# Attention, feed-forward and next-batch projections: from three stages to pieces dealt out between the products of each attention step

## The reference, cut to what matters

```python
# x: (16, 1024, 256), 16 heads of 16 dims; each of the 16 batches stands alone
q, k, v = split_heads(x @ Wq.T + bq), split_heads(x @ Wk.T + bk), split_heads(x @ Wv.T + bv)
scores = einsum('hbnd,hbmd->hbnm', k, q) / 16
attn   = softmax(scores, axis=-1)
out    = einsum('hbnm,hbmd->hbnd', attn, v)
x = layernorm(x + merge_heads(out) @ Wo.T + bo)
gate, up = x @ (w_gate/127).T, x @ (w_up/127).T          # 768 hidden
x = layernorm(x + (silu(gate) * up) @ (w_down/127).T)
```

## Time and profile before

| | |
|---|---|
| median of three runs | 3302.1 us |
| the profiled execution | 3300.9 us |
| its span, first to last instruction | 3299.1 us |
| PE busy | 2933.6 us, 89% |
| ACT busy | 2502.9 us, 76% |
| DVE busy | 1474.3 us, 45% |
| POOL busy | 564.5 us, 17% |
| granted TensorE clock, mean | 0.951 of 2.4 GHz |
| DMA | 145.9 MB, 44 GB/s |

### The profile page before, as it was taken

The page is one execution under the profiler, slowest core; times in us unless marked ns, Lnnn a source line. Parts: engine busy times, 40 slices in busy tenths (PEclk is TensorE's granted clock), DMA queues, the critical chain, the costliest instruction groups (busy, mean ns, idle before and its releaser), DMA issues.

```text
span 3299.1 us, 54053 instructions
## 1 busy us (share of the span) xinstructions
PE 2933.6 (89%) x17577; PEld 1016.6 (31%) x17608; DVE 1474.3 (45%) x2715; ACT 2502.9 (76%) x3013; POOL 564.5 (17%) x672
## 2 busy tenths in 40 slices
PE   4888989898898998989989998898989889898897
PEld 2224142331423324233242422314223142332413
DVE  3344452444534435353453625445344453443535
ACT  1787869778596785968869687795977969678695
POOL 1103021030210203012030210302103021020302
PEclk7999999999999999999999999999999999999998
DMA  3211102011111111111111011110211111111100
GB/s 104 66 37 46 50 31 66 22 57 39 37 60 34 50 34 50 47 34 57 35 49 50 24 61 33 47 50 31 66 34 45 39 47 50 33 50 34 37 21 14
DMA packets 80224, 145.90 MB, mean 44 GB/s; under 512 B 27584, under 2 KB 30272, under 8 KB 75584
## 3 DMA queue, kind: packets, MB, share of 16 engines
q1 hardware_dynamic: 79808, 140.46, 13.2%
HBM read 88.48 MB, written 50.33 MB: 42 GB/s over the span
## 4 chain that ended last, share of the span: by engine, by line
issue 75%; POOL 13%; PE 7%; ACT 3%; DVE 1%; POOLq 1%; DMA 0%; DVEq 0%; SPq 0%; ACTq 0%
PE psum L991 6%; POOL probs L485 6%; POOL squares L452 4%; ACT probs L556 3%; POOL rstd L466 2%; POOL ln_bias L469 1%; PE psum L994 0%; DMA bo_all<-in_L_attn_bo 0%; POOLq L442 0%; POOL xmax_all L443 0%; DVE inv L815 0%; POOL norm_all L459 0%; POOLq L484 0%; DVE wmax L944 0%; ACT parts L520 0%
## 5 line engine op out<-in xcount | busy, mean ns | idle before, releaser
L556 ACT ACTIVATE probs<-psum 128x1024 f32<-128x1024 f32 x2048 | 1973.7, 1026 | 247.8 <-PE psum L991 225.7
L991 PE MATMUL psum<-probs,v 128*32 128x512 f32 x8192 | 1121.7, 622 | 51.5 <-DVE pv L799 49.6
L991 PE MATMUL psum<-kstack,qstack 51*128 51x512 f16 x4096 | 792.6, 398 | 144.4 <-ACT probs L556 102.9
L991 PEld LDWEIGHTS psum<-kstack,qstack 51*128 51x128 f16 x4096 | 193.8, 93 | 1388.3 <-ACT probs L556 981.9
L715 DVE SCALAR_TENSOR_TENSOR parts<-psum,scale_now,parts 128x512 f16<-128x512 f32 x128 | 96.0, 750 | 822.4 <-ACT parts L520 822.4
L991 PEld LDWEIGHTS psum<-probs,v 128*32 128x32 f32 x8192 | 164.8, 109 | 326.7 <-issue 228.8
L452 POOL TENSOR_TENSOR squares<-parts 128x512 bf16<-128x512 f16 x128 | 133.3, 1041 | 771.4 <-DVE parts L715 771.4
L534 ACT ACTIVATE x_res<-x_res,ln_bias,rstd 128x256 f32<-128x256 f32 x256 | 139.9, 596 | 163.0 <-POOL ln_bias L469 163.0
L466 POOL TENSOR_TENSOR rstd<-vareps,minus_half 128x2 f32<-128x2 f32 x128 | 89.3, 698 | 995.8 <-DVE neg_mean L852 995.8
L485 POOL TENSOR_TENSOR probs<-h,probs 128x512 f16<-128x512 f32 x192 | 222.5, 1159 | 196.9 <-ACT probs L592 196.9
L991 PE MATMUL psum<-outT,gateT 128*128 128x512 f16 x768 | 210.7, 399 | 40.2 <-issue 38.8
(11 more groups left out here) (115 smaller groups left out, 2199.9 us busy)
## 6 DMA issues: line engine op xcount, KB each, us to landing
parts_dram<-parts SPq DMA_DIRECT2D x64, 512.0 KB, 2.8
qstack<-parts_dram SPq DMA_DIRECT2D x384, 64.0 KB, 2.1
kstack<-parts_dram SPq DMA_DIRECT2D x384, 64.0 KB, 2.1
x_pre<-in_L_attn_x SPq DMA_DIRECT2D x17, 1024.0 KB, 5.0
x_res<-in_L_attn_x SPq DMA_DIRECT2D x16, 1024.0 KB, 4.8
out<-x_res SPq DMA_DIRECT2D x32, 512.0 KB, 2.7
kstack<-shift_parts SPq DMA_DIRECT2D x384, 4.0 KB, 1.8
probs<-in_L_ffn_w_gate SPq DMA_DIRECT2D x1, 768.0 KB, 9.0
```

The lines of the kernel that those rows point to most:

```text
L556: nc.scalar.activation(probs[:, k % 2, 2 * pr:2 * pr + 2, hf * HALF:(hf + 1) * HALF], scores[u % 2], ACT.Exp, scale=score_scale).then_inc( ...
L991: return nc.tensor.matmul(o, lhsT, rhs, start=start, stop=stop)
```

## The change

The two stages become one. A batch has now 64 steps (4 groups x 2 halves of 512 columns x 8 tiles) of two units each. Per step PE issues, in this order: the two score pairs, the products of the step before (one half, 4 matmuls), and then *pieces* of items. The items of a middle batch b are the whole preparation of batch b+1 (`xT`, `qk`, `norm`, `v`) and the whole of what was `post` of batch b-1 (`out`, `x1T`, `gate`, `up`, `down`), 60 items in a fixed order (`FULL`). `Plan` deals their matmuls to the 64 steps in proportion to a table `COST` (matmuls and ns of each kind). Batch 0 has only the preparation items, batch 15 only the post items of batch 14, and a tail does those of batch 15 alone. `v`, the scales and the softmax scale are doubled by the batch's parity, so the loop body is two batches.

PSUM: banks 0-3 scores, 4-5 accumulators, now one per segment (group, half), 6-7 the ring for all items. The feed-forward has no longer four banks but these two. PE waits at an item's first piece until the item two places before is emptied.

Emptying: everything by DVE, except the first half of `qk` (ACT `hi`, then DVE) and of `gate` (ACT tanh, then DVE). ACT does these extras of step k after both exponentials of step k: for an item that ended in step e, in step e+1. DVE also takes over `xT`, `v`, the fp16 copy in `x1T`, and the four `normalise`. `take_segment` replaces `take_group`: a 32x32 block transpose of the accumulator on DVE, a reciprocal of 128 x 16, a multiplication, and for every odd group a transpose back.

`decide` stands at step 55 and the flag is read by PE at step 57. POOL reduces the maxima at step 55, after the `rstd` of down 2.

The diff, cut to its core:

```diff
-UNITS = HEADS * TILES
-STEPS = GROUPS * TILES
+STEPS = GROUPS * HALVES * TILES
+UNITS = 2 * STEPS
+RINGS = 2
+ACCS = 2
+COST = {"xT": (4, 109), "x1T": (4, 109), "qk": (2, 868), "norm": (1, 216), "v": (4, 434), "out": (4, 434),
+        "gate": (4, 216), "up": (4, 216), "down": (24, 108)}
+FULL = (some("xT", 0, 1, 2, 3) + some("qk", 0, 1, 2, 3) + some("out", 0, 1, 2, 3) + some("qk", 4, 5)
+        + some("norm", 0, 1, 2, 3) + some("x1T", 0, 1) + gate_up(0, 1, 2, 3) + some("x1T", 2, 3)
+        + gate_up(4, 5, 6, 7, 8, 9, 10, 11) + some("qk", 6, 7) + some("norm", 4, 5) + some("down", 0)
+        + some("norm", 6, 7) + some("down", 1, 2, 3) + some("v", 0, 1, 2, 3))
+DECIDE, RELOAD = 55, 57
+class Plan:
+    def __init__(self, items, prepares):
...
+        for n, (kind, _) in enumerate(items):
+            count, cost = COST[kind]
+            steps = [min(STEPS - 1, (at + cost * i + cost // 2) * STEPS // total) for i in range(count)]
...
+            k = max(k, self.ends[n] + (2 if kind in ("qk", "gate") else 1))
+            self.dve[k].append((kind, j, n))
+            if kind == "qk":
+                self.act[self.ends[n] + 1].append((kind, j, n))
+                self.pool[k].append((kind, j, n))
+            elif kind == "gate":
+                self.act[self.ends[n] + 1].append((kind, j, n))
...
 # ACT
+                for k in range(STEPS):
+                    for pr in range(2):
+                        act.wait_ge(scores_ready, UNITS * b + 2 * k + pr + 1)
+                        if pr == 0 and (k >= 2 or not first):
+                            act.wait_ge(pv_done, STEPS * b + k - 1)
+                        nc.scalar.activation(probs[:, k % 2, 2 * pr:2 * pr + 2, :], scores[pr], ACT.Exp,
+                                             scale=score_scale[par]).then_inc(probs_ready, 1)
+                    extras(k)
 # DVE
+            def take_segment(b, s):
...
+                dve.wait_ge(pv_done, STEPS * b + TILES * (s + 1))
+                nc.vector.transpose(flipped[:, hf, :], bank[ACC + s % ACCS]).then_inc(acc_free, 1)
+                dve.drain()
+                nc.vector.reciprocal(inv[:, hf, :], in_block[:, hf, :, sums])
+                dve.drain()
+                nc.vector.tensor_tensor(scaled_block[:, hf, :, at:at + HEAD_DIM], in_block[:, hf, :, at:at + HEAD_DIM],
+                                        inv[:, hf, :].unsqueeze(2).to_broadcast([P, BLOCKS, HEAD_DIM]), ALU.mult)
+                if odd:
+                    dve.drain()
+                    nc.vector.transpose(outT[:, c, hf * HALF:(hf + 1) * HALF], scaled[:, hf, :]).then_inc(out_ready, 1)
 # PE
+            def do_item(plan, n, lo, hi, start, pre, post, w_parts, fresh=False):
+                kind, j = plan.items[n]
+                o = bank[RING + n % RINGS]
+                count = COST[kind][0]
+                if lo == 0 and not (fresh and n < RINGS):
+                    pe.wait_ge(ring_free, start + n - RINGS + 1)
...
+            def batch(b, par, first, last, w_parts):
+                plan = PRE_PLAN if first else POST_PLAN if last else FULL_PLAN
+                for k in range(STEPS):
+                    if k == RELOAD and not last:
+                        pe.wait_ge(flag_ready, b + 2)
+                    score(b, k, first)
...
+                    if k:
+                        products(b, par, k - 1, first)
...
+                    for n, lo, hi in plan.pieces[k]:
+                        do_item(plan, n, lo, hi, base(b), b + 1, b - 1, w_parts)
+            def everything(w_parts):
+                batch(0, 0, True, False, w_parts)
+                with pe.Fori(1, BATCHES - 1, 2) as b:
+                    batch(b, 1, False, False, w_parts)
+                    batch(b + 1, 0, False, False, w_parts)
+                batch(BATCHES - 1, 1, False, True, w_parts)
+                products(BATCHES - 1, 1, STEPS - 1, False)
+                for n in range(len(ONLY_POST)):
+                    do_item(POST_PLAN, n, 0, COST[ONLY_POST[n][0]][0], base(BATCHES - 1) + len(ONLY_POST), None,
+                            BATCHES - 1, w_parts)
```

More of the change, by code:

```diff
@@ L94 @@
 STACK = ROWS + SHIFT_ROWS
-UNITS = HEADS * TILES
-STEPS = GROUPS * TILES
-PREPARE = 4
+STEPS = GROUPS * HALVES * TILES
+UNITS = 2 * STEPS
+SEGMENTS = GROUPS * HALVES
+PER_GROUP = HALVES * TILES
 QK = 8
[L105 to L110, removed]
@@ L142, in taken @@
[L142 to L161, removed]
@@ new lines, in batch, with extras @@
+            def batch(b, par, first, last):
+                plan = PRE_PLAN if first else POST_PLAN if last else FULL_PLAN
+                def extras(k):
+                    for kind, j, n in plan.act[k]:
+                        if kind == "qk":
+                            hi(j, n, base(b), b + 1, 1 - par)
+                        elif kind == "gate":
+                            tanh(plan, j, n, base(b))
+                        else:
+                            h_hi(j, n, base(b))
+                for k in range(STEPS):
[6 more added lines that the diff above has]
+                    extras(k)
+                    if k == ESC_LOAD and not last:
+                        load_scale(1 - par)
+                for k in range(STEPS, len(plan.act)):
+                    extras(k)
@@ new lines, in _ @@
+            act.wait_ge(scale_ready, 1)
+            load_scale(0)
+            for j in range(QK):
+                hi(j, FIRST.index(("qk", j)), 0, 0, 0, True)
+            batch(0, 0, True, False)
+            with act.Fori(1, BATCHES - 1, 2) as b:
+                batch(b, 1, False, False)
+                batch(b + 1, 0, False, False)
+            batch(BATCHES - 1, 1, False, True)
+            start = base(BATCHES - 1) + len(ONLY_POST)
+            for g in range(2 * HCHUNKS):
+                tanh(POST_PLAN, g, POST_PLAN.place("gate", g), start)
+                if g >= 1:
+                    h_hi(g - 1, POST_PLAN.place("up", g - 1), start)
@@ L897, in batch @@
[L897 to L910 removed]
+                at, sums = odd * HEAD_DIM, (1 - odd) * HEAD_DIM
```

892 lines of the change are left out of this document (367 added, 525 removed).

## The result

The changed kernel takes 3698.9 us (median of four runs, 3687.7 to 3706.1), the kernel before 3299.7 beside it: 1.121 times as long, 95% interval 1.119 to 1.123. The forecast was 3605, within 3200 to 3760. The sign and the mechanism came out, and the amount was 94 us short. All medians here are of executions in the usual state; one of the six of experiment 12's kernel, 4456.1 us at a mean clock of 0.555, is left out.

The account below looks back on a forecast made before the run. The prediction took PE as the bound. Work 171.8, waits 42.1, loop end 1.0 and clock 10 made 224.9 us per middle batch; 14 of these plus 456 us of ends gave 3605 us, range 3200 to 3760.

Parts of the forecast that it names:

- PE's work at full clock: Middle batch: attention steps 103.7 us plus item pieces 68.1 us, 171.8 us of matmuls if nothing waited.
- ring waits, gate stage: Steps 22 to 42: PE waits for gate banks to be emptied, some behind take_segment, 23.9 us per middle batch.
- other waits: Steps 0, 19, 20, 38, 46 and 49: PE waits for copies, norms and extras, 13.4 us per middle batch.
- flag: Before step 57's scores: PE waits behind POOL's reduction and DVE's compare, 4.8 us per middle batch.
- loop end: Loop end every two batches costs some 2 us of issue, 1.0 us per batch.
- the clock: Middle batch: PE's work slows at 1.2 GHz around waits, 10 us taken from between 0 and 17.
- the twelve steps: Steps 22 to 42: each loses 1.3 to 2.05 us to a gate or x1T bank wait, 20.7 us together.
- The transposes: DVE in take_segment: 0.7 us taken from the shuffle's row, bounds 0.5 and 1.4, skill-based estimate 1.24.
- rival with full clock: Whole kernel: same waits, but the array stays at 2.4 GHz, giving 3465 us; chance 0.22.
- cold gate stage: Steps 19 to 49: low clock throughout, unstalled steps 4.9 instead of 2.7 us, giving 3844 us; chance 0.17.
- rival of covered waits: Middle batches: ACT and DVE empty the ring earlier; half covered 3169 us, all 2875; chances 0.14 and 0.04.
- The ends: Outside the middle batches: start 96.8, batch 0 136, batch 15 152, tail 71 us, together 456 us.

Follow-up runs that it names:

- experiment 12: Changed kernel with three ring banks, one accumulator, both POOL reductions earlier, another item order, tanh before the exponentials, flag read at step 58: 3032.5 us, ratio 0.919.
- Experiment 1: Changed kernel with ACT's tanh of gate items moved ahead of the step's two exponentials: 3573.9 us, ratio 1.083.
- experiment 2: Changed kernel with three ring banks and one accumulator bank instead of two and two: 3301.4 us, ratio 1.000.
- Experiment 11: Changed kernel with one accumulator bank, ring of two, plus useless matmuls ahead of nine ring waits: 3640.8 us, ratio 1.105; without these matmuls 3705.5 us.
- experiment 10: Changed kernel's two ring and two accumulator banks, with both POOL reductions earlier, another item order and tanh before the exponentials: 3401.6 us, ratio 1.031.

## Why the prediction was right, and where it was short

By its own steps, for a middle batch:

| | predicted | measured |
|---|---|---|
| PE's work at full clock | 171.8 | 172.6 |
| ring waits, gate stage | 23.9 | 21.1 |
| other waits | 13.4 | 11.7 |
| flag | 4.8 | 4.5 |
| loop end | 1.0 | 1.9 |
| the clock | 10 | 17.0 |
| batch | 224.9 | 228.8 |

The measured waits are PE's idle time between the two flag loads, divided by 14; step 28's wait of about 1.0, which the list puts down to an `x1T` copy, is with the ring waits, where the prediction has it. For the work, the same matmuls in the fastest kernel (experiment 12) serve as the measure:

```profile
229.30:2776.70 2547.40, 2441.94 (x15317) 764.75 (x15319) 1089.41 (x2284) 1958.80 (x2240) 467.35 (x461) 0.99 0.15 48
```

That is 174.4 us busy per batch at a clock of 0.99, so some 1.8 us of it are still from the low clock, and 172.6 is left. The changed kernel's 189.4 is 16.8 above that; with rounding, 17.0 closes the table. The granted clock gives nearly the same: 0.93 over 228.8 us is 14% of it, 32 us, at the lower level, and 16 us lost if all of that falls on work.

**The work** was right: 172.6 against 171.8, and experiment 12's kernel, at 182.0 per batch, comes near it. One reading beside it was not: PE's idle time before was put down mostly to layernorm and the flag, but its list of waits has the exponentials first (102.9 us, "issue" 73.0, the accumulators at the flag 49.6, layernorm 35.8). Nothing in the sum hangs on it.

**The ring waits** came out as counted: +3.67 us of the step, the twelve steps, and the longer waits behind `take_segment` (2.73 and 3.05). Experiment 1 shows that they need the tanh's place and experiment 2 that they need the ring of two. The sum is 2.8 us too high: step 33, behind the longest wait, lost only 0.70 and step 28 only 1.02, less than the 1.3 counted for the shortest, and step 40's even segment was done nearly when its tanh was, so that it waited 1.53, no longer than steps without one.

**The transposes.** The changed kernel shows 0.72 us for 128x512, as I took from the shuffle's row:

```profile
L783 DVE STREAM_TRANSPOSE flipped<-psum 128x512 f32<-128x512 f32 x128 | 91.7, 716 | 326.6 <-PE psum L897 326.4
```

The Trainium skill, page "VectorE: DVE Perf Modes", section "The three transpose paths", led to an estimate of 1.24 us, four times its figure for 128x128 in bf16, which is also for 32x32 blocks. The measurement decides: 0.72 for 128x512 fp32.

**The flag.** The chain stood as predicted, and took the place of the 3.12 of the earlier trace rows. The prediction's own terms add up to 9.4 us from the start of step 55, not to its 9.9; measured, PE goes on at +9.6:

```profile
1370.62 0.37 POOL L441 PARTITION_ALL_REDUCE norm_all<-norm_safe  x1 [5.92 <-issue]
...
1371.37 0.16 DVE L735 TENSOR_TENSOR flag<-over,scales 128x1 int32<-128x1 f32 x1
...
1371.67 1.03 PE L897 MATMUL psum<-kstack,qstack 51*128 51x512 f16 x4 [4.30 <-DVE flag L735]
```

**The clock is the term that was mis-sized.** I took 10 out of 0 to 17, arguing that half of the low stretches lie inside the waits. They hardly do: the low clock comes behind a wait and covers the work there. In the wait of step 32 the granted clock (third from the end) is still 1.00, and in the products behind it 0.50:

```profile
1284.00:1285.30 1.30, 0.00 (x0) 0.00 (x0) 1.27 (x2) 0.00 (x0) 0.00 (x0) 1.00 0.54 136
1287.00:1288.00 1.00, 1.00 (x8) 0.20 (x8) 1.00 (x1) 0.56 (x1) 0.00 (x0) 0.50 0.00 0
```

(In the kernel before, the clock fell inside the wait of 3.12: it is 0.50 in the last 0.9 us of it.) The 34 us of low clock were forecast well (32 measured), and they cost 16 to 17 us, the upper end; 7 more than I took are 98 us in all. Experiment 11 shows 6.1 of them directly, at nine waits; the rest rests on the granted clock and on the comparison with experiment 12. The length of a wait does not alone say what follows: behind 2.12 us in step 26 the next products took 1.06 us, behind 1.88 in step 27 they took 1.94:

```profile
1259.46 1.04 PE L897 MATMUL psum<-ffn,gateT 128*128 128x512 f16 x4 [2.12 <-DVE tanh_out L660]
...
1261.18 1.06 PE L897 MATMUL psum<-probs,v 128*32 128x512 f32 x8
...
1264.88 0.55 PE L900 MATMUL psum<-ident,x_res 128*128 128x128 f32 x3 [1.88 <-DVE tanh_out L660]
...
1266.32 1.94 PE L897 MATMUL psum<-probs,v 128*32 128x512 f32 x8
```

The rival with full clock (3465) is refuted, as is the cold gate stage: the products of steps 29 to 32, between waits of 1.02, 1.80 and 3.05, took 1.06 or 1.07.

**The rival of covered waits** needs ACT and DVE to empty the ring before PE returns. They don't, because ACT's tanh waits behind exponentials whose scores PE has just made. Yet the conditions under which it comes true lie near: with a third ring bank, another item order, POOL's two reductions moved, the tanh first and a later flag, 3032.5. The Trainium skill, page "Perfetto Trace Analysis", section "Matmul Optimizations", asks for matmuls back to back. The changed kernel mixes them with waits and loses. Experiment 11, 65 us faster with matmuls in place of waiting, agrees with it, and so does the kernel of experiment 12, with PE busy 95.9% between the two flag loads (2441.94/2547.40). What the prediction cites beside it, that the matmul engine be kept as utilised as possible, stands in the section "Optimization Strategies" of that page of the Trainium skill.

**The ends** were 484 in place of 456. Measured by the first scores of batches 1 and 15 (246.05 and 3455.59) and the last products (3612.60): start 97.6 (96.8), batch 0 148.4 (136), batch 15 157.0 (152), tail 80.8 (71). In batch 0 I summed PE's work alone, but with few pieces a step is shorter on PE than two exponentials on ACT. Such waits are 10.0 of the 16.4 us above the 132 of that sum (4 were allowed for), as the list of PE's waits in batch 0 shows:

```profile
PE psum L897 <- ACT probs L551: 10.0, 22, 0.5
```

The tail's excess is one wait that I did not see at all, out 2 behind out 0's addition. Its input is loaded only when the results of batch 14 are stored (at 3618.97), and then POOL adds the bias for 4.49 us:

```profile
3629.14 3.35 PE L897 MATMUL psum<-WoT,outT 128*128 128x256 f32 x7 [11.83 <-DVE x_res L684]
```

Cut by first scores, a middle batch is (3455.59 - 246.05)/14 = 229.25 us. The misses add up: 28 for the ends and 14 x (229.25 - 224.9) = 61, together the 89 by which the span's 3693.4 exceeds the sum's 3604.6. The clock alone is 98; the waits and the loop end give 3.9 us a batch back, and the work takes 0.8.

## What to carry to other kernels

When work is threaded into an in-order engine's queue, count for each ring bank the time from fill to free through every queue it passes, and compare it with the step: one bank more in the ring was worth 361 to 404 us, and the same bank as a second accumulator, beside a ring of two, nothing that could be measured. Waits hide one another: removing the largest showed the next (POOL's first reduction, then the runs of short items, then the transpose behind POOL's second), so re-read the list of waits after every edit, and don't add up single gains: the item order was worth 134 us with three banks and, by the sum of experiment 10, none with two. A placement is read by what stands behind it: the reduction of the maximum, with which POOL is taken for 13 us, cost 97 us more at one step than fourteen steps earlier.

## What the runs showed of the hardware

Behind a wait of 2.73 us the array ran at the lower clock for the work of about one step (products 1.93 in place of 1.06 us), behind one of 1.58 it did not; between them the length did not decide (2.12 without, 1.88 with). Matmuls whose result nobody reads, put in place of the waiting, made the kernel 65 us faster.

POOL's reduction over the partitions has 5.9 to 6.0 us of issue before its 0.37 us of execution on 1 or 2 columns, and POOL's next instruction starts another 6.83 (experiment 1) or 7.55 us (experiment 12) behind it, though its input is there.
